# Graph attention kernel: runs of 3225, a pick list and gathers issued early, and two sender columns of 75 fetched row by row by SyncE and ScalarE

## The reference

```python
h = relu(layernorm(x))
msg = silu(silu(e@W1+b1)@W2+b2) * sigmoid(silu(e@G1+g1)@G2+g2)   # e: edge features
x = x + h + segment_sum(msg, dst)
h = relu(layernorm(x))
s, r = h@Ws + bs, h@Wr + br                                      # 4 heads x 16
logits = mish(s[src] + r[dst]) . aw + ab                         # per edge and head
alpha = softmax of logits over the edges of one receiver
x = x + segment_sum(alpha * s[src], dst)
```

## Time and profile before

| | |
|---|---|
| median of 3 runs | 5629.94 us (5627.07 to 5633.66) |
| the profiled execution | 5634.19 us |
| its span, first to last instruction | 5632.3 us |
| busy: VectorE, GpSimd, ScalarE, TensorE | 4318.9, 3651.0, 2923.2, 1122.9 us |
| indirect DMAs `se` from `s_proj` in attention | 3196 |
| single rows fetched by SyncE | 5632 |

### The profile page before, as it was taken

The page is one execution under the profiler, slowest core; times in us unless marked ns, Lnnn a source line. Parts: engine busy times, 40 slices in busy tenths (PEclk is TensorE's granted clock), DMA queues, the critical chain, the costliest instruction groups (busy, mean ns, idle before and its releaser), DMA issues. The chain is left out here.

```text
span 5632.3 us, 62352 instructions
## 1 busy us (share of the span) xinstructions
PE 1122.9 (20%) x8383; PEld 507.6 (9%) x8383; DVE 4318.9 (77%) x3980; ACT 2923.2 (52%) x3415; POOL 3651.0 (65%) x3705
## 2 busy tenths in 40 slices
PE   7989999923000000000000000000000000000000
PEld 3333344412000000000000000000000000000000
DVE  6888877754388878888787888878888887887871
ACT  7888899911244444444444444444444444444440
POOL 3555300067677777777777777777777777777756
PEclk9999999955555555555555555555555555555555
DMA  7778877721323333233323323333233332333222
GB/s 214 245 243 249 257 251 252 250 56 43 64 75 87 86 87 86 75 87 87 84 79 85 86 76 86 86 87 87 75 87 87 86 80 82 86 87 79 82 61 49
DMA packets 316507, 631.77 MB, mean 112 GB/s; under 512 B 116870, under 2 KB 120264, under 8 KB 315843
## 3 DMA queue, kind: packets, MB, share of 16 engines
q1 hardware_dynamic: 195714, 502.89, 27.7%
q0 software_dynamic: 118384, 126.30, 11.5%
q10 hardware_dynamic: 2128, 0.23, 0.1%
HBM read 392.85 MB, written 236.18 MB: 112 GB/s over the span
## 5 line engine op out<-in xcount | busy, mean ns | idle before, releaser
L915 POOL DMA_INDIRECT se<-s_proj,idx x3124 | 2951.2, 945 | 952.6 <-issue 940.1
L933 ACT ACTIVATE held_ps<-keepf 128x1536 f32 (+1 forms) x135 | 196.3, 1454 | 1402.4 <-DVE z L1022 1361.5
L1158 PE MATMUL a_ps<-r_ident,r_state 128*4 128x128 f32 x1 | 0.4, 374 | 4073.9 <-DVE drop L1187 4073.9
L1022 DVE TENSOR_TENSOR z<-se,held_ps 128x1536 f32<-128x1536 f32 x135 | 369.6, 2738 | 401.1 <-DMA se<-s_proj,idx 362.9
L984 ACT ACTIVATE arows<-work_ps 128x1632 f32<-128x1632 f32 x135 | 206.8, 1532 | 741.4 <-DVEq L1058 741.4
L1047 DVE TENSOR_TENSOR wse<-se,ex_ps 128x1536 f32<-128x1536 f32 x135 | 373.9, 2769 | 205.5 <-ACT ex_ps L975 205.5
L413 DVE TENSOR_TENSOR_SCAN sums<-keepb,sums,msg 128x1024 f32<-128x1024 bf16 x201 | 472.6, 2351 | 31.3 <-DVE msg L404 26.8
L1055 DVE TENSOR_TENSOR_SCAN work_ps<-work_ps,wse 128x1632 f32<-128x1632 f32 x135 | 481.3, 3565 | 4.7
L335 ACT ACTIVATE hidden<-h_ps,r_b1g 128x1024 f32<-128x1024 f32 x404 | 458.7, 1136 | 15.3 <-PE h_ps L280 15.3
L1014 DVE TENSOR_TENSOR_SCAN held_ps<-held_ps,rnew 128x1536 f32<-128x1536 f32 x135 | 454.3, 3365 | 4.6
L291 PE MATMUL v_ps<-hidden,r_w2g 64*64 64x512 f32 x1616 | 441.7, 615 | 15.1 <-issue 3.5
(11 more groups left out here) (190 smaller groups left out, 4184.1 us busy)
## 6 DMA issues: line engine op xcount, KB each, us to landing
states<-arows SPq DMA_DIRECT2D x135, 864.0 KB, 6.8
rs<-sums SPq DMA_DIRECT2D x135, 768.0 KB, 5.1
edges<-in_edge_attr SPq DMA_DIRECT2D x202, 512.0 KB, 4.4
sums<-rows SPq DMA_DIRECT2D x402, 256.0 KB
fetched<-s_proj SPq DMA_DIRECT2D x5632, 0.2 KB
keepb<-keep SPq DMA_DIRECT2D x404, 128.0 KB, 3.4
se<-s_proj,idx POOLq DMA_INDIRECT x3124
r_base<-in_x POOLq DMA_DIRECT2D x1, 3136.0 KB, 12.9
```

The source lines that it names most:

```text
L915: pool.indirect_dma_start(out=se[b][:, k, :], out_offset=None, in_=D["s_proj"], in_offset=bass.IndirectOffsetOnAxis(ap=node[:, k:k + 1], a ...
L1022: nc.vector.tensor_tensor(z[b][:, :, :], se[b][:, :, :].rearrange("p k f -> p f k"), rneg, ALU.subtract).then_inc(z_ready, 1)
```

## The change

- T = 25 instead of 30, so RUN = 3225 instead of 3240. With TA = 25 there are 129 chunks and 43 iterations instead of 135 and 45. `keep` in DRAM gets 298 more elements by a second small store.
- COLS = 2 columns of the 75 of an iteration are fetched row by row, 256 rows: SyncE fetches 192 in 12 pieces of 16, four pieces to a chunk; ScalarE fetches the last 64 rows of the second column in 8 pieces of 8.
- The node numbers are loaded from `src` in DRAM straight into a tile `picks` of 8 partitions by 94 strided loads in `update_nodes`; the way over DRAM is gone, and with it the block's wait for it.
- The first 8 gathers of the first chunk are issued at the end of `update_nodes`, behind the scatters and before the wait for them. Their buffer and semaphore live across both blocks.
- ex_ps moves into the fourth PSUM bank of `held_ps`.

```diff
-T = 30
+T = 25
-TA, B = 24, 3
+TA, B = 25, 3
-PICK, GANG = 1, 8
+EARLY = 8
+BEYOND = E2 + NBLK * BLK - P * RUN
+PICK, GANG, COLS = 1, 16, 2
+SHARE = P - 64
+PIECES = [(n, g) for n in range(COLS) for g in range(P // GANG) if n == 0 or g * GANG < SHARE]
@@ edge_mlp, sync
-            sp.dma_start(D["keep"].rearrange("(p k) -> p k", p=P), keep16[:, :]).then_inc(keep_out, 16)
-            sp.wait_ge(keep_out, 16)
+            sp.dma_start(D["keep"][0:P * RUN].rearrange("(p k) -> p k", p=P), keep16[:, :]).then_inc(keep_out, 16)
+            sp.dma_start(row(D["keep"][P * RUN:]), keep16[P - 1:P, RUN - BEYOND:RUN]).then_inc(keep_out, 16)
+            sp.wait_ge(keep_out, 32)
@@ update_nodes, sync
+            for i in range(CA // B):
+                for n in range(COLS):
+                    column = A["src"][(i * B + PICK + 1) * TA - COLS + n::RUN]
+                    even = column.shape[0] // GANG
+                    sp.dma_start(R["picks"][0:even, i, n, :], column[0:even * GANG].rearrange("(g q) -> g q", q=GANG), allow_slow_non_contiguous=True)\
+                        .then_inc(picks_in, 16)
...
-            picked = R["src"][:, :].rearrange("p (i c k) -> p i c k", c=B, k=TA)[:, :, PICK, TA - 1]
-            sp.dma_start(D["picks"].rearrange("i p -> p i"), picked, allow_slow_non_contiguous=True).then_inc(picks_out, 16)
-            sp.wait_ge(picks_out, 16)
+            sp.wait_ge(picks_in, 16 * COLS * (2 * (CA // B) - LAST // B))
@@ update_nodes, gpsimd
+            for b in range(2):
+                pool.wait_ge(tabled[b], 16 * (NS // 2))
+            for k in range(EARLY):
+                pool.indirect_dma_start(out=R["se0"][:, k, :], out_offset=None, in_=D["s_proj"],
+                                        in_offset=bass.IndirectOffsetOnAxis(ap=R["src"][:, k:k + 1], axis=0)).then_inc(gathered0, 16)
@@ attention, sync
-            def fetch(i, gangs):
+            def fetch(i, pieces):
...
+                for n, g in pieces:
+                    first = g * GANG
+                    size = GANG if n == 0 else min(GANG, SHARE - first)
+                    sp.reg_load(nodes[0:size], R["picks"][g:g + 1, bass.ds(i, 1), n, 0:size].rearrange("a i q -> a (i q)"))
+                    for q in range(size):
+                        node = sp.snap(nodes[q], min_val=0, max_val=NN - 1)
+                        sp.dma_start(fetched[first + q:first + q + 1, n, :], D["s_proj"][bass.ds(node, 1), :]).then_inc(fetched_in, 16)
...
-                        fetch(i + 1, range(P // GANG * b // B, P // GANG * (b + 1) // B))
+                        fetch(i + 1, PIECES[len(PIECES) * b // B:len(PIECES) * (b + 1) // B])
@@ attention, gpsimd
-                for k in range(TA if first or b != PICK else TA - 1):
+                for k in range(EARLY if first and b == 0 else 0, TA if first or b != PICK else TA - COLS):
@@ attention, scalar
+            def fetch(i, at):
+
+                g, q0 = at // GANG, at % GANG
+                act.reg_load(nodes, R["picks"][g:g + 1, bass.ds(i, 1), COLS - 1, q0:q0 + 8].rearrange("a i q -> a (i q)"))
+                for q in range(8):
+                    node = act.snap(nodes[q], min_val=0, max_val=NN - 1)
+                    act.dma_start(fetched[at + q:at + q + 1, COLS - 1, :], D["s_proj"][bass.ds(node, 1), :]).then_inc(fetched_in, 16)
...
                     mish_tail(c)
+                    if not last:
+                        if b == 0 and not first:
+                            act.wait_ge(placed, i)
+                            act.sem_inc(act_turn, 1)
+                        fetch(i + 1, SHARE + b * 24)
+                        fetch(i + 1, SHARE + b * 24 + 8)
...
-                        act.wait_ge(fetched_in, i * (16 * P) + 16 * P)
-                        nc.scalar.activation(se[b2][:, TA - 1, :], fetched[:, :], ACT.Copy).then_inc(placed, 1)
+                        act.wait_ge(fetched_in, i * (16 * P * COLS) + 16 * P * COLS)
+                        nc.scalar.activation(se[b2][:, TA - COLS:TA, :], fetched[:, :, :], ACT.Copy).then_inc(placed, 1)
...
+                    if not last and b < 2:
+                        fetch(i + 1, SHARE + b * 24 + 16)
                     act.wait_ge(summed, c + 1)
```

More of the change, by code:

```diff
@@ L35 @@
 NBLK = -(-E2 // BLK)
-PAD_P = 111
+PAD_P = 100
 PAD = (P * RUN - E) // PAD_P * F
@@ L572, in _, with update_nodes @@
             pool.wait_ge(x_in, 16)
-def update_nodes(nc, R, A, D):
+def update_nodes(nc, R, A, D, gathered0):
     with ExitStack() as ctx:
@@ L609, in update_nodes @@
         src_in = sem("src_in")
-        picks_out = sem("picks_out")
+        picks_in = sem("picks_in")
         centered = sem("centered")
@@ L634, in _ @@
             sp.dma_start(R["src"][P - 1:P, 0:LAST * T], A["src"][(P - 1) * RUN:E].rearrange("(a k) -> a k", a=1)).then_inc(src_in, 16)
+            sp.wait_ge(padded, 2)
+            for i in range(CA // B):
[4 more added lines that the diff above has]
+                        .then_inc(picks_in, 16)
+                    if column.shape[0] < P:
+                        sp.dma_start(R["picks"][even:even + 1, i, n, 0:GANG - 1], column[even * GANG:P - 1].rearrange("(g q) -> g q", g=1),
+                                     allow_slow_non_contiguous=True).then_inc(picks_in, 16)
             for k in range(NS):
@@ L740, in _ @@
             nc.vector.memset(R["src"][96:P, LAST * T:RUN], 0).then_inc(padded, 1)
+            nc.vector.memset(R["picks"][:, :, :, :], 0).then_inc(padded, 1)
             pairs = [slice(2 * JB * k, 2 * JB * (k + 1)) for k in range(NS // 2)]
@@ L767, in _, with attention @@
             project(NS - 1)
-def attention(nc, R, A, D):
+def attention(nc, R, A, D, gathered0):
     with ExitStack() as ctx:
@@ L782, in attention @@
         idx = [sb(f"idx{b}", [P, TA], i32) for b in range(B)]
-        se = [sb(f"se{b}", [P, TA, F]) for b in range(B)]
+        se = [R["se0"]] + [sb(f"se{b}", [P, TA, F]) for b in range(1, B)]
         rs = [sb(f"rs{b}", [P, TA, F]) for b in range(B)]
@@ L804, in attention @@
         heads = sb("heads", [P, F])
-        picks = sb("picks_tile", [1, CA // B, P], i32)
-        fetched = sb("fetched", [P, F])
+        fetched = sb("fetched", [P, COLS, F])
         rows = [sb(f"arows{b}", [P, TA, ROW]) for b in range(B)]
-        held_ps, work_ps, ex_bank = ps("held_ps", [P, 3 * 512]), ps("work_ps", [P, 4 * 512]), ps("ex_ps", [P, 512])
+        held_ps, work_ps = ps("held_ps", [P, 4 * 512]), ps("work_ps", [P, 4 * 512])
+        ex_bank = held_ps[:, F * TA:(F + H) * TA]
         rneg = held_ps[:, 0:F * TA].rearrange("p (f t) -> p f t", t=TA)
@@ L811, in attention @@
         num = work_ps[:, 0:H * HE * TA].rearrange("p (h e t) -> p h e t", h=H, e=HE)
-        ex_ps = ex_bank[:, 0:H * TA].rearrange("p (h t) -> p h t", h=H)
-        picks_in = sem("picks_in")
+        ex_ps = ex_bank.rearrange("p (h t) -> p h t", h=H)
         fetched_in = sem("fetched_in")
@@ L822, in attention @@
         sp_turn = sem("sp_turn")
-        gathered = [sem(f"agathered{b}") for b in range(B)]
+        act_turn = sem("act_turn")
+        gathered = [gathered0] + [sem(f"agathered{b}") for b in range(1, B)]
         rs_in = [sem(f"rs_in{b}") for b in range(B)]
@@ L847, in landed @@
         def landed(i, b):
-            columns = TA - 1 if b == PICK else TA
+            columns = TA - COLS if b == PICK else TA
             return i * (16 * columns) + 16 * TA
@@ L894, in _ @@
             load(0, 0)
-            sp.wait_ge(picks_in, 16)
             body(0, first=True)
@@ L955, in mish_tail @@
                 nc.scalar.activation(act_ps, t1[:, :, :], ACT.Exp, scale=-1.0).then_inc(r_ready, 1)
+            nodes = [act.alloc_register(f"own_node{g}") for g in range(8)]
+            def fetch(i, at):
[4 more added lines that the diff above has]
+                    act.dma_start(fetched[at + q:at + q + 1, COLS - 1, :], D["s_proj"][bass.ds(node, 1), :]).then_inc(fetched_in, 16)
             def body(i, first=False, last=False):
@@ L974, in body @@
                     act.wait_ge(exin_ready, c + 1)
-                    nc.scalar.activation(ex_bank[:, 0:H * TA], exin[:, :], ACT.Exp).then_inc(ex_ready, 1)
+                    nc.scalar.activation(ex_bank, exin[:, :], ACT.Exp).then_inc(ex_ready, 1)
                     nc.scalar.activation(dec[:, :], decin[:, :], ACT.Exp).then_inc(dec_ready, 1)
@@ L1235, in gnn_program @@
     D = {
-        "keep": nc.dram_tensor("keep", [P * RUN], bf16).ap(),
+        "keep": nc.dram_tensor("keep", [E2 + NBLK * BLK], bf16).ap(),
         "samples": nc.dram_tensor("samples", [S1, S2], i32).ap(),
@@ L1240, in gnn_program @@
         "states": nc.dram_tensor("states", [P * RUN, ROW], f32).ap(),
-        "picks": nc.dram_tensor("picks", [CA // B, P], i32).ap(),
         "s_proj": nc.dram_tensor("s_proj", [NN, F], f32).ap(),
@@ L1250, in gnn_program @@
             "head": ([P, 1], i32), "mend": ([P, 1], i32), "mcol": ([P, 1], i32), "mhot": ([P, 1], f32), "cont": ([P, 1], f32),
```

(7 more changed lines are left out.)

1 line of the change is left out of this document (removed).

## The result

The changed kernel takes 6390.48 us (median of 4 runs, 6387.97 to 6398.26), the kernel before 5628.7 (4 runs, 5627.07 to 5633.66): a ratio of 1.135 (95% interval 1.133 to 1.137). It is **slower by 13.5%**, where 7.5% was forecast: the direction and the bound were right, but 6390 lies above the range, which ended at 6340.

The account below looks back on a forecast made before the run. SyncE's row fetching was to replace GpSimd as the bound at 103.4 us an iteration: 1573 + 41 x 103.4 (4239) + 242 = 6054, adjusted to 6052 us for the median, 7.5% slower; range 5890 to 6340.

Parts of the forecast that it names:

- SyncE's iteration: 90.9 + 8.3 + 4.2: Attention loop: three thirds, two inner gaps and the gap over `placed` make 103.4 us, above GpSimd's 91.2.
- The two rivals: Attention loop: GpSimd stays the bound, 5552 us, chance 0.06; or ScalarE becomes the bound, 6730 us, chance 0.11.
- The third: SyncE's 64 rows in four loads of 16, a third of its iteration: 30.3 us instead of 24.77.
- the case "double" (+0.69): Upper bound for SyncE's 16-register load: twice the 8-register load's cost, +0.69 us instead of the 0.15 taken.
- The gaps inside: Two gaps between thirds, with a load of `rs` and a store of `states`: 8.3 us for both.
- The gap over `placed`: Iteration's end, until ScalarE has copied the fetched rows: landing, copy, way to the first row, about 4.2 us.
- the landing: Arrival of the last fetched row before ScalarE's copy: taken as 2.4 us, 1.5 in the range's lower case.
- The first copy: First `placed` copy, before the 41 iterations counted: 5 us earlier, at 1573 instead of 1577.9.
- the tail: From the last `placed` copy to the kernel's end: stays 242 us.
- The early gathers and the pick list: Node update: block's end put where it was, pick-list loads nothing; as a rival 10 to 30 us more.
- The range: Whole kernel: 5890 to 6340 us, from the forecast's bounds and a little of ScalarE's case.
- ScalarE's rival: Attention loop: ScalarE's row issues become the bound, 120 us an iteration at 0.97 a row, 6730 us; chance 0.11.

Follow-up runs that it names:

- one_column_no_early: The one_column kernel without the eight early gathers (EARTLY 8 set to 0 as EARLY = 0): 5597.2 us, 0.994 of the kernel before.
- sync_160: Changed kernel with SyncE fetching 160 rows and ScalarE 96 in twelve pieces: 5967.5 us, 101.5 us an iteration.
- combined: Changed kernel with sync_160, registers_first and loop_by_two together: 5880.7 us, 1.044 of the kernel before.
- loads_of_8: Changed kernel with each piece of 16 rows loaded in two register loads of 8: 6439.7 us.
- registers_first: Changed kernel with the first register load of each third ahead of the load of rs and the store of states: 6143.5 us.
- loop_by_two: Changed kernel with two iterations in SyncE's hardware loop: 6349.9 us where the kernel before takes 5632.0; 9386.7 and 9330.7 on the other chip.
- one_column: Changed kernel with one column fetched by SyncE, none by ScalarE; runs of 3225, pick list and early gathers stay: 5594.9 us, 0.994 of the kernel before.

## Why the prediction was right in kind and wrong in size

- **The bound.** "SyncE's iteration: 90.9 + 8.3 + 4.2", above GpSimd's 91.2: right. The wait turned round as forecast, and taking 48 rows away gives the 91.2 back. The two rivals fell for this kernel: the row's pitch is SyncE's own (a third is 31 us, not under 26), and ScalarE's 64 issues cost nothing.
- **The third, 30.3 us forecast, 31.0 measured.** The row was right (225 ns, pitch 0.42). The load of 16 registers was put at 0.15 us over one of 8; it takes 1.14 instead of 0.69, 0.45 more, which is 57 ns a register between 8 and 16. My line went through VectorE's load of one register and SyncE's of eight, two engines. The measured value lies between the one taken and the case "double" (+0.69). For three thirds that makes 2.0 us an iteration.
- **The gaps inside, 8.3 forecast, 11.2 measured.** I added 0.15 us to each old gap. The register load in it stands behind two large transfers; the old row gave its largest value, 2.69 us for 8 registers, and I read only the median. With 16 it is up to 4.39. Worth 2.9 us.
- **The gap over `placed`, 4.2 forecast, 8.3 measured: the step that failed most.** I priced the chain landing, copy, first row, and called it "no less than the other gaps". (Its terms add up to 3.95, and I wrote "about 4.2".) But the queue has its own work in the same place: the jump, the load, the store and the slow register load. The copy began 1 us after the last row's issue had ended, so the landing, put at 2.4 us, was shorter than that term, and SyncE did not wait for the copy in the loop. The jump's pause stood in the trace before: the third that began at 3047.80 ended at 3072.57, and the next load of `rs` was issued at 3075.59, while the steady stage has only 4.0 us of waits for `carried` in all. These two rows of before, from its queue's timeline and its waits, I did not use:

```profile
3075.59 0.38 SPq L858 DMA_DIRECT2D rs<-sums  x1
...
SPq L858 <- DVE rnew L1011: 4.0, 11, 0.9
```

  Between these two thirds lie 16.5 us (3072.57 to 3089.09), and the longest wait for `placed` is 12.1: at least 4.4 us of that gap were the queue's own work, even with a load of 8 registers. Worth 4.0 us.
- **Together** 8.9 us by the iteration shown, 8.6 by the average of all; times 41 that is 351 us. The first copy (1566.7, forecast 1573) and the tail (239.3, forecast 242) take 9 away, and the 342 left are what the profiled execution (6398.26) has over the forecast's 6056.
- **The early gathers and the pick list: nothing, right by luck.** From the first load of the update to the barrier are 286.7 us before and 286.1 after, but two effects nearly cancel in it. The drain, which I named, grows by 8.7 us. And GpSimd's last scatter of before, issued at 1423.00, was followed by the drain only at 1437.2; with the pick list (one_column_no_early) it is 1411.78 and 1414.2, 11.8 us less. Before, SyncE's store of the picked numbers, issued at 1415.52, took until about 1436 to land:

```profile
1415.52 0.56 SPq L640 DMA_DIRECT2D picks<-r_src  x1
...
picks<-r_src SPq DMA_DIRECT2D x1, 22.5 KB, 20.4
```

  That this store held up GpSimd's wait for its scatters is likely by these times, but no run has the pick list alone. The 94 loads of the pick list were mis-sized too: 0.76 us a piece instead of 0.42, so 71 us of SyncE's issue (1156.1 to 1227.2) instead of 40.
- **The range.** Its top was built from one doubled load. The jump and the slow load behind the transfers had no upper bound in it, though no row of before showed a 16-register load or an iteration's end without a wait.
- **ScalarE's rival** had the right sum and the wrong price. It gave 120 us at 0.97 a row and 97.6 at 0.62, prices from the kernel's first microseconds; in the loop of the changed kernel ScalarE's rows begin 0.39 us apart in the median. For 96 rows in twelve pieces the same sum gives 101.5 us at 0.42 (98.4 at 0.39), where sync_160 took 101.5 and combined 99.8.

## What to carry to other kernels

Before work is moved into an engine's spare time, add up that engine's whole iteration, with jump, register loads and the instructions around its waits; a wait in which it also does other work is shorter than the gap in which it is seen. Take a price from the row with the same neighbours (a register load behind large transfers is not one between rows), and give it its own upper bound. Where a bound changes hands, a little too much costs far more than the right share brings: 48 rows in 256 here were 15% of the kernel's time, while the best complete kernel here is 0.6% faster than the kernel before.

## What the runs showed of the hardware

- A register load takes 0.69 us for 8 registers and 1.14 for 16; directly behind the issue of two large transfers up to 2.64 and 4.39, on average 2.0 and 3.9 (loads_of_8 and the changed kernel). Put ahead of them the load of 16 takes 1.14, and the row's issue behind them up to 1.5 (registers_first).
- With a jump back in SyncE's loop the next instruction comes 2.5 us later (0.31 us without, 2.82 with, in loop_by_two); each jump less saved 1.9 us of the kernel.
- Eight software gathers ahead of a barrier lengthen GpSimd's drain from 9.2 to 17.9 us; nothing is won by issuing them there (one_column and one_column_no_early).
- One chip of the same kind runs the kernel before at 8750 instead of 5630 us. In the changed kernels' traces there, single instructions of SyncE's and ScalarE's queues take up to 1.4 us, with pauses of 0.5 to 1 us between them; the median instruction is as fast as elsewhere.
